# Graph network and mixture of experts on one core: column sums of the late rows in PSUM columns of their own, projections taken earlier, four gate transfers a batch, and the last routing in parts

## The chip, the core and the metric

The kernel runs on one core of a Trainium2 chip. The core has five engines that run side by side and meet only at semaphores: PE (TensorE, matrix products and transposes into PSUM), DVE (VectorE), ACT (ScalarE), POOL (GpSimd) and SP (SyncE, which here only issues transfers). The metric is the device time of one execution in microseconds; lower is better.

## The reference, cut to what matters

```python
# x: (8, 2048, 128), adj: (2048, 2048), 8 experts, the best 2 of them per token
z = layernorm(x)                       # no scale, no shift
A = relu((adj + adj.T) * 0.5)
D = A.sum(axis=1)                      # degrees: row sums of a symmetric matrix
d = where(D > 0, where(D > 0, D, 1) ** -0.5, 0)
x = x + relu((I - d[:, None] * A * d[None, :]) @ (z @ W))
z = layernorm(x)
probs = softmax(z @ router_w.T);  rw, re = top_k(probs, 2);  rw = rw / max(rw.sum(-1), 1e-12)
combine = zeros(N, 8); combine[arange, re] = rw
x = x + z + sum over e of combine[:, e] * (gelu(z @ w1[e] + b1[e]) @ w2[e] + b2[e])
```

All is float32; the kernel splits operands into a high and a low float32r part and makes three products for each one.

## The kernel before, in words

`adj` is cut into 16 x 16 blocks of 128 x 128. Only the lower triangle of the symmetric matrix is kept, in the tile `s_tri` (136 blocks). The program has three stages, and the code of each engine is a list written out by hand; what stands earlier in an engine's list blocks what stands later.

**Setup** walks over the block rows j = 15 down to 0 (r = 0 to 15 in the code, so j = 15 - r). For each row SP loads the row and the column of `adj` (`low`, `up`, in three large buffers and later six half ones; a buffer is loaded again when the row named in `FREED_BY` has been summed). PE transposes the column blocks into PSUM (`turn`), DVE adds the loaded row (`add`, L715), and ACT takes the relu and, with it, the row sums (`relu`, L607). The degrees also need the sums over columns: POOL adds the blocks of rows 14 to 5 into `col_sum` (`add_columns`, L572), and PE turns them into column sums with products of one column (`column_sum`): one with row 15's block, one with `col_sum`, and one for each of the rows 4 to 1 (L671, L675, L679). Between the rows stand 16 jobs of projection: PE transposes a piece of `x` (`turn_x`, L322), ACT copies it (`copy_x`, L328), PE multiplies it by W (`project`, L341) and ACT keeps the result (`keep`, L353), while DVE takes its statistics. The list `JOBS` says how many jobs a row has. `project(k)` waits for `keep(k-2)`, since there are two PSUM buffers. In ACT's list a row's jobs copy ahead of its relus and keep behind them. When the degrees are known in three parts (`degrees`, `root`), ACT and DVE scale the projections into `y_high` (L614) and `y_low` (L742), and the first stage tile is made (`turn_group` L445, `high_group` L452, `low_group` L459).

**Graph** has 32 units (two halves of the batch, 16 block columns each). In a unit PE makes 16 x 3 products of 512 columns (L957 to L959), and between them small work for other units. In the first half units 8 to 15 also carry the projections of the second half, two jobs each. In the second half the operand tile `stage` is read back from DRAM (L861 on SP). Each unit's result is normalised (DVE, POOL), transposed (`turn_z`, L901), split and stored, and routed: PE gives logits, and each four units make one of eight batches, in which DVE picks the best two experts (`pick`, 12 instructions) and weighs them (`weigh`, 10 instructions). The gates then go to DRAM with `store_gates`, 16 transfers a batch (L840). Seven batches are on SP's queue, in units 7, 11, 15, ..., 31, between the loads and stores of the units; the last one is on POOL's.

**Experts** has 32 units of 8 experts. PE makes three products up and three down for each expert (L1317 to L1333), ACT the gelu (L1369) and the high part (L1376), DVE the gate and the low part (L1407, L1412). Its order is software pipelined: `down_product` runs three experts behind. The end of the graph stage's last unit is put between the first experts by `graph_tail`, which looks up the count of experts t in `tail_tensor`, `tail_scalar` and `tail_vector`.

## Time and profile before

| | us |
|---|---|
| median of 3 runs (lowest, highest) | 934.3 (929.2, 935.61) |
| the profiled execution | 933.2 |
| its span (first to last instruction) | 931.5 |
| PE busy | 874.6 (94%) |
| DVE busy | 634.3 (68%) |
| ACT busy | 499.3 (54%) |
| POOL busy | 306.5 (33%) |

The profiled execution took 933.2 us, of which 1.7 lie outside the span. Shares over the span are means over three stages with different limits; the windows of each stage say more. Setup ends and the graph stage begins at 87 us; the experts begin at 539 us.

### The profile page before, as it was taken

Reading aid. Unit: us, or ns where it says so; the run is one execution under the profiler, and the core shown is the slowest. Engines: PE = TensorE matmul, PEld = TensorE weight load, DVE = VectorE, ACT = ScalarE, POOL = GpSimd, SP = SyncE. Lnnn points to the kernel's source line nnn. Section 1 sums busy time; section 2 is a strip of 40 time slices with the busy share of each in tenths; the row PEclk is TensorE's granted clock in tenths of the full one; section 3 lists DMA queues with packets and bytes.
Section 4 is the critical chain, followed back from the end, with each engine's and each line's share of the span. In section 5 each row is a group of like instructions: output and inputs, shape, how many; then the busy total and the mean of one; then the engine's idle time right before and its main releaser. Section 6 shows DMA issues by size and latency. Waiting matters only on the chain.

```text
span 931.5 us, 15186 instructions
## 1 busy us (share of the span) xinstructions
PE 874.6 (94%) x4338; PEld 730.2 (78%) x4338; DVE 634.3 (68%) x1567; ACT 499.3 (54%) x903; POOL 306.5 (33%) x324
## 2 busy tenths in 40 slices
PE   3788999999998999999899988999999999999996
PEld 3688788887786788778687866888888888888885
DVE  3686545657857743252333359999999999999996
ACT  2686423333333311121111168888888888888885
POOL 1792253463664644474244444000000000000000
PEclk9996999999999999999899999999999999999999
DMA  9992366566665356776657865777777777767771
GB/s 284 314 307 104 115 257 260 226 201 215 237 208 196 105 174 248 228 293 219 234 216 284 299 241 176 283 282 276 277 278 280 273 279 271 287 265 279 271 282 51
DMA packets 104477, 222.98 MB, mean 239 GB/s; under 512 B 20888, under 2 KB 71792, under 8 KB 92528
## 3 DMA queue, kind: packets, MB, share of 16 engines
q1 hardware_dynamic: 98848, 212.97, 65.3%
q0 software_dynamic: 3072, 8.59, 2.4%
q10 hardware_dynamic: 2512, 0.86, 0.4%
q8 instruction: 23, 0.38, 0.2%
q14 instruction: 22, 0.18, 0.1%
HBM read 157.89 MB, written 64.49 MB: 239 GB/s over the span
## 4 chain that ended last, share of the span: by engine, by line
PE 61%; issue 12%; POOL 8%; DVE 6%; SPq 5%; DMA 4%; ACT 4%; DVEq 0%; ACTq 0%; POOLq 0%
PE bank L1333 6%; PE bank L1317 6%; PE bank L1319 6%; PE bank L1330 6%; PE bank L1318 6%; PE bank L1331 6%; PE bank L957 5%; PE bank L959 5%; PE bank L958 5%; SPq L840 4%; POOL z L1026 4%; PE bank L341 2%; DMA x_raw<-in_x 2%; POOL rstd L1021 2%; PE bank L1339 1%
## 5 line engine op out<-in xcount | busy, mean ns | idle before, releaser
L1369 ACT ACTIVATE act_h<-bank,b_sb 128x512 f32<-128x512 f32 x256 | 176.2, 689 | 52.2 <-PE bank L1319 47.3
L1407 DVE TENSOR_TENSOR gated<-c_all,act_h 128x512 f32<-128x512 f32 x256 | 176.1, 688 | 33.8 <-ACT act_h L1369 27.9
L1412 DVE TENSOR_TENSOR g_lo<-gated,g_hi 128x512 fp32r<-128x512 f32 x256 | 175.0, 684 | 0.2
L1376 ACT ACTIVATE g_hi<-gated 128x512 fp32r<-128x512 f32 x256 | 159.2, 622 | 4.2 <-DVE gated L1407 4.1
L1301 POOL DMA_DIRECT2D out<-fin x32 | 24.5, 764 | 325.9 <-DVE fin L1420 309.9
L957 PE MATMUL bank<-y,stage 128*128 128x512 f32 x256 | 105.2, 411 | 6.2 <-DMA stage<-s_scratch 6.2
L1021 POOL TENSOR_TENSOR rstd<-var_eps,neg_half 128x4 f32<-128x4 f32 x32 | 48.9, 1527 | 179.0 <-DVE var_eps L1063 178.6
L957 PE MATMUL bank<-y_hi,stage 128*128 128x512 f32 x256 | 107.0, 418 | 0.8 <-DVE y_lo L742 0.8
L1026 POOL TENSOR_SCALAR z<-x,mv,rstd 128x128 f32<-128x128 f32 x128 | 105.2, 837 | 3.4
L978 ACT ACTIVATE z_t<-bank 128x512 f32<-128x512 f32 x32 | 19.1, 598 | 160.9 <-PE bank L901 160.9
L1317 PE MATMUL bank<-z_e,w_hi 128*128 128x512 f32 x256 | 103.3, 403 | 1.4 <-ACT act_h L1369 1.4
L1333 PE MATMUL bank<-g_lo,w_hi 128*128 128x512 f32 x256 | 100.9, 394 | 3.5 <-DVE g_lo L1412 3.5
L959 PE MATMUL bank<-y,stage 128*128 128x512 f32 x256 | 101.6, 397 | 0.0
L959 PE MATMUL bank<-y_hi,stage 128*128 128x512 f32 x256 | 101.2, 395 | 0.0
L958 PE MATMUL bank<-y,stage 128*128 128x512 f32 x256 | 101.2, 395 | 0.0
L1330 PE MATMUL bank<-g_hi,w_lo 128*128 128x512 f32 x256 | 100.6, 393 | 0.0
L1319 PE MATMUL bank<-z_e,w_lo 128*128 128x512 f32 x256 | 100.6, 393 | 0.0
L958 PE MATMUL bank<-y_lo,stage 128*128 128x512 f32 x256 | 100.5, 393 | 0.0
L1331 PE MATMUL bank<-g_hi,w_hi 128*128 128x512 f32 x256 | 100.2, 391 | 0.0
L1318 PE MATMUL bank<-z_e,w_hi 128*128 128x512 f32 x256 | 100.2, 391 | 0.0
L1067 DVE TENSOR_TENSOR z_hl<-z_t,z_hl 128x512 fp32r<-128x512 f32 x32 | 22.2, 693 | 93.5 <-ACT z_hl L981 93.5
L957 PEld LDWEIGHTS bank<-y,stage 128*128 128x128 f32 x256 | 49.2, 192 | 16.6 <-DMA stage<-s_scratch 7.5
(124 smaller groups left out, 1534.2 us busy)
## 6 DMA issues: line engine op xcount, KB each, us to landing
c_all<-c_scratch SPq DMA_DIRECT2D x64, 1024.0 KB, 8.2
s_scratch<-stage SPq DMA_DIRECT2D x14, 2048.0 KB, 8.4
stage<-s_scratch SPq DMA_DIRECT2D x14, 2048.0 KB, 8.5
z_e<-z_scratch SPq DMA_DIRECT2D x32, 512.0 KB, 7.4
z_scratch<-z_hl SPq DMA_DIRECT2D x31, 512.0 KB, 2.7
x_raw<-in_x SPq DMA_DIRECT2D x32, 256.0 KB, 8.2
x_res<-in_x SPq DMA_DIRECT2D x32, 256.0 KB, 7.4
r_e<-res_scratch SPq DMA_DIRECT2D x32, 256.0 KB, 2.7
```

The source lines that it names most:

```text
L957: pe.matmul(out[:, :], s_hi, y_hi, start=(i == 0), stop=False)
L958: pe.matmul(out[:, :], s_hi, y_lo, start=False, stop=False)
L959: last = pe.matmul(out[:, :], s_lo, y_hi, start=False, stop=(i == MB - 1))
L1317: pe.matmul(ps_h[k][:, :], v.w1_hi[:, e, :], v.z_e[s][:, 0, :], start=True, stop=False)
L1318: pe.matmul(ps_h[k][:, :], v.w1_hi[:, e, :], v.z_e[s][:, 1, :], start=False, stop=False)
L1319: pe.matmul(ps_h[k][:, :], v.w1_lo[:, e, :], v.z_e[s][:, 0, :], start=False, stop=True).then_inc(h_done, 1)
L1330: pe.matmul(ps_o[s][:, :], v.w2_lo[:, e, :], hi[:, :], start=False, stop=False)
L1333: pe.matmul(ps_o[s][:, :], v.w2_hi[:, e, :], lo[:, :], start=False, stop=(e == E - 1)).then_inc(o_done, 1)
L1369: act.activation(v.act_h[e % R][:, :], ps_h[e % 2][:, :], ACT.Gelu, bias=v.b1_sb[:, e:e + 1]).then_inc(gelu_done, 1)
L1376: act.activation(v.g_hi[e % R][:, :], v.gated[e % R][:, :], ACT.Copy).then_inc(hi_done, 1)
L1407: dve.tensor_tensor(out=v.gated[e % R][:, :], in0=v.c_all[s][:, e, :], in1=v.act_h[e % R][:, :], op=ALU.mult).then_inc(gated_done, 1)
L1412: dve.tensor_tensor(out=v.g_lo[e % R][:, :], in0=v.gated[e % R][:, :], in1=v.g_hi[e % R][:, :].bitcast(FP32), op=ALU.subtract).then_inc(lo ...
```

## The change

- Setup: `JOBS` takes two projection jobs in rows r = 4 and 5 as well and none in 10 and 11, so that all 16 are issued by the tenth row. The stage tile's first groups move up by one row (r = 11 and 12), and `y_high`'s first ones too.
- Column sums: `LAST` goes from 5 to 9. POOL no longer adds rows 8 to 5; instead each of the rows 8 to 1 gets a one-column product of its own, into its own PSUM column (`row_sums`), and DVE adds up the columns (`deg_col`). The two products with row 15 and `col_sum` are made early (`BASES`).
- Gates: `store_gates` sends four transfers a batch, each with all four units. So that the rows in DRAM are contiguous, the tokens of a unit are stored in another order: `z_hl` is written, and the result read back, through `by_group` and `by_tile`.
- The seam between graph and experts: `turn_z` of the last unit moves from t = 5 to 7, and the last batch's `pick` and `weigh` are cut in eight parts at t = 15, 19, ..., 43. Six units instead of two are written out (`KNOWN`), and POOL stores the last gates behind unit 5.

```diff
-    LAST = 5
-    EARLY_AT = ((15, 14), (13, 12))
-    EARLY = 4
+    LAST = 9
+    EARLY_AT = ((15, 14), (13, 12), (11, 10))
-    JOBS = [2, 2, 2, 2, 1, 1, 1, 1, 1, 1, 1, 1, 0, 0, 0, 0]
+    JOBS = [2, 2, 2, 2, 2, 2, 1, 1, 1, 1, 0, 0, 0, 0, 0, 0]
-    ps_d = [v.banks[2], v.banks[7], v.banks[4]]
+    ps_d = v.banks[2]
+    ps_k = [v.banks[4 if k < 3 else 7][:, k * LAST:(k + 1) * LAST] for k in range(8)]
+    BASES = {8: (7, 6), 9: (5, 4), 10: (3,), 11: (2, 1, 0)}
...
+        def row_sums(j, a, b):
+            pe.wait_ge(relued, until_row(j))
+            for k in range(a, min(j, b)):
+                last = pe.matmul(ps_k[k][:, LAST - j:LAST - j + 1], s_tri[:, block(j, k), :], v.one_col[:, :],
+                                 start=True, stop=True)
+            last.then_inc(row_done, 1)
...
-            if j + 2 < MB:
+            if j + 2 >= 8 and j + 2 < MB:
                 column_sum(j + 2)
-            if r == 12:
+            for k in BASES.get(r, ()):
+                column_sum(k)
+            if 4 <= j + 2 < LAST:
+                row_sums(j + 2, 3, 8)
+            if r == 11:
+                for i in (8, 7, 6):
+                    row_sums(i, 0, 3)
+            if r >= 12:
+                row_sums(j + 2, 0, 3)
+            if r == 10:
                 pr.project(pe, MB - 1)
+            if r == 11:
                 pe.wait_ge(deg_step, 2)
                 pe.wait_ge(pr.hw_kept, MB - 1)
                 for g in range(2):
                     st.turn_group(pe, 0, g)
...
-        column_sum(1)
-        column_sum(0)
+        row_sums(1, 0, 3)
...
+                dve.tensor_reduce(out=v.deg_col[:, a:b], in_=v.banks[7 if p == 1 else 4][:, a * LAST:b * LAST].rearrange(
+                    "p (k i) -> p k i", i=LAST), axis=AX.X, op=ALU.add).then_inc(deg_step, 1)
...
+            if r == 10:
+                dve.wait_ge(pr.xt_copied, MB)
+                dve.memset(v.banks[4][:, 0:3 * LAST], 0.0).then_inc(zeroed, 1)
...
     def store_gates(eng, batch):
         eng.wait_ge(gate_turned, batch + 1)
-        for u in range(4 * batch, 4 * batch + 4):
-            rows = v.c_dram[unit(u)].rearrange("e (q g t) -> g e q t", q=Q, g=4)
-            for g in range(4):
-                eng.dma_start(rows[g], v.gate_x[32 * g:32 * g + 3 * E, Q * (u % 4):Q * (u % 4) + Q, :]).then_inc(
-                    gate_last if batch == U // 4 - 1 else gate_out[half(u)], 16)
+        w = min(unit(4 * batch), unit(4 * batch + 3))
+        rows = v.c_dram[w:w + 4].rearrange("w e (g c) -> g e w c", g=4)
+        for g in range(4):
+            eng.dma_start(rows[g], v.gate_x[32 * g:32 * g + 3 * E, :, :].rearrange(
+                "e (w q) t -> e w (q t)", q=Q)).then_inc(gate_last if batch == U // 4 - 1 else gate_out[half(4 * batch)], 16)
...
-            act.activation(v.z_hl[:, 0, :], v.z_t[:, :], ACT.Copy).then_inc(z_hi_done, 1)
+            act.activation(v.by_group(v.z_hl[:, 0, :]), v.by_tile(v.z_t[:, :]), ACT.Copy).then_inc(z_hi_done, 1)
...
-            act.activation(v.o_t[:, :], ps_o[s][:, :], ACT.Copy).then_inc(ot_copied, 1)
+            act.activation(v.by_tile(v.o_t[:, :]), v.by_group(ps_o[s][:, :]), ACT.Copy).then_inc(ot_copied, 1)
...
-        v.tail_tensor = {5: [(turn_z, U - 1)], 7: [(route, U - 1)]}
+        v.tail_tensor = {7: [(turn_z, U - 1)], 10: [(route, U - 1)]}
-        v.tail_scalar = {6: [(copy_z, U - 1)], 8: [(store_last, U - 1)], 9: [(exps, 7)]}
+        v.tail_scalar = {8: [(copy_z, U - 1)], 12: [(store_last, U - 1)], 17: [(exps, 7)]}
-        v.tail_vector = {6: [(z_low, U - 1)], 8: [(copy_logits, U - 1), (pick, 7)], 10: [(weigh, 7)]}
+        v.tail_vector = {9: [(z_low, U - 1)], 11: [(copy_logits, U - 1)], 15: [(largest, 7, 0)], 19: [(first_of, 7, 0)],
+                         23: [(largest, 7, 1)], 27: [(first_of, 7, 1)], 31: [(add_picked, 7)], 35: [(weigh, 7)],
+                         39: [(split_gate, 7)], 43: [(turn_gates, 7)]}
```

Three places show how instructions move. The first is PE's list from the fifth row's transposes to the seventh's in setup (`up` x11 is row r = 4). Before:

```order
L341 MATMUL bank<-gnn_w_sb,x_t_115 128x128 x4
L662 MATMUL bank<-ident,up_101 128x128 x11
L662 MATMUL bank<-ident,low_100 128x128
L671 MATMUL bank<-one_col,s_tri 128x1
L675 MATMUL bank<-one_col,col_sum 128x1
L322 MATMUL bank<-ident,x_raw_111 128x128 x4
L341 MATMUL bank<-gnn_w_sb,x_t_114 128x128 x4
L662 MATMUL bank<-ident,up_103 128x128 x10
```

The same place with the change (L325 and L344 are `turn_x` and `project`, L673 is `turn`):

```order
L344 MATMUL bank<-gnn_w_sb,x_t_116 128x128 x4
L325 MATMUL bank<-ident,x_raw_112 128x128 x4
L344 MATMUL bank<-gnn_w_sb,x_t_115 128x128 x4
L673 MATMUL bank<-ident,up_101 128x128 x11
L673 MATMUL bank<-ident,low_100 128x128
L683 MATMUL bank<-one_col,s_tri 128x1
L687 MATMUL bank<-one_col,col_sum 128x1
L325 MATMUL bank<-ident,x_raw_113 128x128 x4
L344 MATMUL bank<-gnn_w_sb,x_t_116 128x128 x4
L325 MATMUL bank<-ident,x_raw_114 128x128 x4
L344 MATMUL bank<-gnn_w_sb,x_t_115 128x128 x4
L673 MATMUL bank<-ident,up_103 128x128 x10
```

A second transpose and projection stands ahead of row 4's transposes, and again ahead of row 5's.

The second place is the end of setup on PE, from the last transpose to the first large product. Before:

```order
L662 MATMUL bank<-ident,low_102 128x128
L671 MATMUL bank<-one_col,s_tri 128x1
L675 MATMUL bank<-one_col,col_sum 128x1
L679 MATMUL bank<-one_col,s_tri 128x1 x2
L671 MATMUL bank<-one_col,s_tri 128x1
L675 MATMUL bank<-one_col,col_sum 128x1
L679 MATMUL bank<-one_col,s_tri 128x1 x3
L671 MATMUL bank<-one_col,s_tri 128x1
L675 MATMUL bank<-one_col,col_sum 128x1
L679 MATMUL bank<-one_col,s_tri 128x1 x4
L957 MATMUL bank<-y_hi,stage_96 128x512
```

With the change (L694 is `row_sums`):

```order
L673 MATMUL bank<-ident,up_103 128x128
L673 MATMUL bank<-ident,low_102 128x128
L694 MATMUL bank<-one_col,s_tri 128x1 x3
L673 MATMUL bank<-ident,low_102 128x128
L694 MATMUL bank<-one_col,s_tri 128x1 x3
L999 MATMUL bank<-y_hi,stage_96 128x512
```

Fifteen one-column products behind the last transpose become three. The others stand earlier: behind the transposes of row r = 11 and ahead of the first `turn_group` there are now 18 (six for `BASES` and twelve in a row of `row_sums`, L694), where two stood behind those of row r = 12.

The third place is SP's list in unit 7 of the graph stage, around the first batch of gates. Before:

```order
L269 DMA x_raw_110<-in_x 128x4x128
L269 DMA x_raw_111<-in_x 128x4x128
L840 DMA c_scratch<-gate_x 96x1x32 x16
L869 DMA res_scratch<-res 128x512
L872 DMA z_scratch<-z_hl 128x1024
L853 DMA s_scratch<-stage_96 128x4096
```

With the change:

```order
L272 DMA x_raw_111<-in_x 128x4x128
L272 DMA x_raw_112<-in_x 128x4x128
L882 DMA c_scratch<-gate_x 24x4x128 x4
L911 DMA res_scratch<-res 128x512
L914 DMA z_scratch<-z_hl 128x1024
L895 DMA s_scratch<-stage_96 128x4096
```

Four transfers take the place of sixteen, with the same 96 pieces each, and each piece four times as long.

## Rows read from the trace of the kernel before

**Rows 1.** The page: granted clock of PE in 40 equal slices, in tenths of full speed.

```profile
PEclk9996999999999999999899999999999999999999
```

**Rows 2.** Windows: busy us (x instructions) of PE, PEld, DVE, ACT, POOL; clock, DMA share, GB/s.

```profile
446.00:453.00 7.00, 5.67 (x14) 4.47 (x15) 4.42 (x19) 0.00 (x0) 2.37 (x3) 0.51 1.02 419
...
551.50:555.50 4.00, 4.00 (x12) 3.10 (x12) 1.95 (x3) 2.87 (x5) 0.66 (x1) 0.57 1.01 406
...
600.00:900.00 300.00, 300.00 (x1374) 248.26 (x1373) 274.91 (x441) 259.89 (x441) 19.35 (x26) 1.00 0.75 276
```

**Rows 3.** Timeline of PE in the graph stage: start, us, instruction, idle before it.

```profile
219.28 1.16 PE L341 MATMUL bank<-gnn_w_sb,x_t 128*128 128x128 f32 x8 [1.16 <-ACT x_t L328]
...
286.98 1.16 PE L341 MATMUL bank<-gnn_w_sb,x_t 128*128 128x128 f32 x8 [2.05 <-ACT x_t L328]
...
304.20 1.16 PE L341 MATMUL bank<-gnn_w_sb,x_t 128*128 128x128 f32 x8 [1.54 <-ACT x_t L328]
...
393.22 0.50 PE L957 MATMUL bank<-y,stage 128*128 128x512 f32 x1 [1.22 <-DMA stage<-s_scratch]
...
447.32 0.80 PE L957 MATMUL bank<-y,stage 128*128 128x512 f32 x1 [3.55 <-DMA stage<-s_scratch]
...
500.80 0.80 PE L957 MATMUL bank<-y,stage 128*128 128x512 f32 x1 [1.38 <-DMA stage<-s_scratch]
```

**Rows 4.** Timeline of SP's queue in the graph stage.

```profile
188.48 13.95 SPq L840 DMA_DIRECT2D c_scratch<-gate_x  x16
...
205.10 4.20 SPq L269 DMA_DIRECT2D x_raw<-in_x  x2
...
421.84 13.28 SPq L840 DMA_DIRECT2D c_scratch<-gate_x  x16
...
436.20 0.45 SPq L861 DMA_DIRECT2D stage<-s_scratch  x1
```

**Rows 5.** Timeline of DVE in setup, the adds of rows r = 2 to 5 and 10.

```profile
33.30 2.22 DVE L715 TENSOR_TENSOR s_tri<-bank,low 128x512 f32<-128x512 f32 x4 [3.05 <-PE bank L662]
...
40.50 2.08 DVE L715 TENSOR_TENSOR s_tri<-bank,low 128x512 f32<-128x512 f32 x4 [2.13 <-PE bank L662]
...
46.23 1.89 DVE L715 TENSOR_TENSOR s_tri<-bank,low 128x512 f32<-128x512 f32 x3 [2.22 <-PE bank L662]
49.47 1.74 DVE L715 TENSOR_TENSOR s_tri<-bank,low 128x512 f32<-128x512 f32 x3
...
66.89 1.02 DVE L715 TENSOR_TENSOR s_tri<-bank,low 128x512 f32<-128x512 f32 x2 [0.36 <-PE bank L662]
```

**Rows 6.** Timeline of PE at the end of setup.

```profile
85.37 1.84 PE L679 MATMUL bank<-one_col,s_tri 128*128 128x1 f32 x8
87.07 0.77 PE L957 MATMUL bank<-y_hi,stage 128*128 128x512 f32 x1
```

**Rows 7.** Timeline at the seam: PE, ACT, DVE and POOL.

```profile
550.84 0.65 PE L901 MATMUL bank<-ident,z 128*128 128x128 f32 x4 [3.03 <-POOL z L1026]
...
564.77 0.50 PE L1333 MATMUL bank<-g_lo,w_hi 128*128 128x512 f32 x1 [2.57 <-DVE g_lo L1412]
...
560.05 1.28 ACT L985 ACT_TABLE_LOAD   x1
...
553.11 0.69 DVE L1407 TENSOR_TENSOR gated<-c_all,act_h 128x512 f32<-128x512 f32 x1 [3.61 <-ACT act_h L1369]
...
559.65 0.29 DVE L1084 TENSOR_REDUCE top<-logits 128x16 f32<-128x128 f32 x1
...
563.42 0.69 DVE L1407 TENSOR_TENSOR gated<-c_all,act_h 128x512 f32<-128x512 f32 x1
...
544.10 6.68 POOL L1026 TENSOR_SCALAR z<-x,mv,rstd 128x128 f32<-128x128 f32 x4
```

**Rows 8.** The page: two groups over the whole span: busy us, mean ns of one.

```profile
L1376 ACT ACTIVATE g_hi<-gated 128x512 fp32r<-128x512 f32 x256 | 159.2, 622 | 4.2 <-DVE gated L1407 4.1
...
L1026 POOL TENSOR_SCALAR z<-x,mv,rstd 128x128 f32<-128x128 f32 x128 | 105.2, 837 | 3.4
```

More of the change, by code:

```diff
@@ L586, in gpsimd @@
                     pr.scale_kept(pool, k)
-            if 4 <= r < 12:
+            if r >= 4 and jobs(r):
                 pr.invert(pool, jobs(r))
@@ L666, in column_sum @@
             pe.wait_ge(relued, until_row(MB - 1))
-            if part_of(k) == 2:
-                pe.wait_ge(pr.xt_copied, MB)
-            out = ps_d[part_of(k)][:, k:k + 1]
+            if k in (7, 2):
+                pe.wait_ge(zeroed, 3 if k == 7 else 4)
+            out = ps_d[:, k:k + 1] if k >= 8 else ps_k[k][:, 0:1]
             if k < MB - 1:
@@ L1106, in weigh, with largest @@
-        def weigh(batch):
+        choices = ((v.logits, v.is_1st), (v.others, v.is_2nd))
+        def largest(batch, n):
+            values, k = choices[n][0], STEPS * batch + 6 * n
+            if n == 0:
+                dve.wait_ge(logits_copied, 4 * batch + 4)
+            dve.tensor_reduce(out=v.top[:, :], in_=values[:, :, :], axis=AX.X, op=ALU.max).then_inc(route_step, 1)
+            dve.wait_ge(route_step, k + 1)
+            if n == 0:
+                wait(dve, exp_done, batch)
+                dve.tensor_tensor(out=v.shifted[:, :, :], in0=values[:, :, :], in1=spread(v.top),
+                                  op=ALU.subtract).then_inc(shift_done, 1)
+            dve.tensor_tensor(out=v.same[:, :, :], in0=values[:, :, :], in1=spread(v.top),
+                              op=ALU.is_equal).then_inc(route_step, 1)
@@ new lines, in first_of @@
+        def first_of(batch, n):
+            (values, chosen), k = choices[n], STEPS * batch + 6 * n
+            dve.wait_ge(route_step, k + 2)
+            dve.tensor_tensor(out=v.key[:, :, :], in0=v.same[:, :, :], in1=v.rev_iota[:, :, :],
+                              op=ALU.mult).then_inc(route_step, 1)
+            dve.wait_ge(route_step, k + 3)
+            dve.tensor_reduce(out=v.top_key[:, :], in_=v.key[:, :, :], axis=AX.X, op=ALU.max).then_inc(route_step, 1)
+            dve.wait_ge(route_step, k + 4)
+            dve.tensor_tensor(out=chosen[:, :, :], in0=v.key[:, :, :], in1=spread(v.top_key),
+                              op=ALU.is_equal).then_inc(route_step, 1)
+            dve.wait_ge(route_step, k + 5)
+            if n == 0:
+                dve.scalar_tensor_tensor(out=v.others[:, :, :], in0=chosen[:, :, :], scalar=-3.0e38, in1=values[:, :, :],
+                                         op0=ALU.mult, op1=ALU.add).then_inc(route_step, 1)
+                dve.wait_ge(route_step, k + 6)
@@ L1107, in weigh, with add_picked @@
+        def add_picked(batch):
             first = STEPS * batch + STEPS_A
@@ L1116, in weigh @@
             dve.tensor_reduce(out=v.sum_top[:, :], in_=v.picked[:, :, :], axis=AX.X, op=ALU.add).then_inc(route_step, 1)
+        def weigh(batch):
+            first = STEPS * batch + STEPS_A
             dve.wait_ge(route_step, first + 3)
@@ L1122, in weigh, with split_gate @@
             dve.wait_ge(route_step, first + 5)
+            wait(dve, gate_turned, batch)
+            dve.tensor_tensor(out=v.gate_parts[:, :, 0:E], in0=v.picked[:, :, :], in1=spread(v.inv_top),
+                              op=ALU.mult).then_inc(route_step, 1)
+        def split_gate(batch):
             gate, high, low = (v.gate_parts[:, :, i * E:(i + 1) * E] for i in range(3))
-            wait(dve, gate_turned, batch)
-            dve.tensor_tensor(out=gate, in0=v.picked[:, :, :], in1=spread(v.inv_top), op=ALU.mult).then_inc(route_step, 1)
-            dve.wait_ge(route_step, first + 6)
+            dve.wait_ge(route_step, STEPS * batch + STEPS)
             dve.tensor_copy(high.bitcast(FP32R), gate)
@@ L1132, in weigh, with pick, share @@
             if batch > 4:
-                dve.wait_ge(gate_out[1], 256 * (batch - 4))
+                dve.wait_ge(gate_out[1], 64 * (batch - 4))
             else:
-                wait(dve, gate_out[0], 256 * batch)
+                wait(dve, gate_out[0], 64 * batch)
             dve.transpose(v.gate_x[:, :, :].rearrange("p t c -> p (t c)"),
                           v.gate_parts[:, :, :].rearrange("p t c -> p (t c)")).then_inc(gate_turned, 1)
+        def pick(batch):
+            for n in range(2):
+                largest(batch, n)
+                first_of(batch, n)
+        def share(batch):
+            add_picked(batch)
+            weigh(batch)
+            split_gate(batch)
+            turn_gates(batch)
         for u in range(U):
@@ L1172, in graph_tail @@
 def graph_tail(parts, t):
-    for part, u in parts.get(t, []):
-        part(u)
+    for part, *of in parts.get(t, []):
+        part(*of)
 def expert_stage(nc, sem, v):
@@ L1243, in over_units @@
     def over_units(eng, body):
-        for s in range(2):
-            body(0, s, s)
-        with eng.Fori(1, U // 2) as h:
+        for u in range(KNOWN):
+            body(u // 2, u % 2, u)
+        with eng.Fori(KNOWN // 2, U // 2) as h:
             for s in range(2):
```

98 lines of the change are left out of this document (43 added, 55 removed).

## The prediction

> **What bounds the kernel now.** I read the windows first. From 600 to 900 us PE is busy without a gap at full clock, DVE for 274.9 of the 300 us and ACT for 259.9 [rows 2]. This third of the time can only get longer by the change, so any gain lies before it. The page's clock line [rows 1] has its lowest slice, 6, as the fourth, from 70 to 93 us, and a single 8 near 460; the timeline of PE then shows where it waits. In the graph stage it waits for two things: for an x_t copy of ACT, 1.16, 2.05 and 1.54 us, and for a stage tile that is still being read, 1.22, 3.55 and 1.38 us [rows 3]. SP's queue shows why: the sixteen gate transfers hold it for 13.95 and 13.28 us, and the load of x_raw at 205.10 and the load of the stage tile at 436.20 stand right behind them [rows 4]. At the seam PE waits 3.03 us for POOL's z and 2.57 us for a low part that DVE makes late [rows 7]. In setup no engine is full; the rows follow each other in a chain, and the last thing is PE's own column sums [rows 5, 6].
>
> **Gate transfers.** A batch takes SP 13.95 us for sixteen, 0.87 each; four take 3.5, so 10.4 us of the queue come free in each of seven batches, if a transfer keeps its price. Its pieces are as many as before and four times as long; by the nearest row, the load of a whole stage tile issues in 0.45 us [rows 4], so length doesn't set the price. Bounds: 0.45 to 3.5 us for one, at which nothing would be saved; I take 0.87.
> - Stage loads: the three loads come 10 us earlier, more than the longest wait. All three waits go: 1.22 + 3.55 + 1.38 = 6.15 us.
> - The clock: after the 3.55 us wait the granted clock is 0.51, the lower of the two levels (1.2 GHz), with 5.67 us of PE busy in 7 us [rows 2]. That work takes half as long at the upper level, 2.8 us. A second, shorter such stretch follows the wait at 500.80; its first product takes 0.80 us against a normal one's 0.4 or 0.5, and I put it at 1.6 us. Together 4.4; bounds 0 and 4.4, as nothing else idles PE there.
> - Projections of units 8 to 15: the waits of 1.16 and 2.05 us stand in the units right behind a batch, where x_raw is late. They go: 3.2 us. The 1.54 us wait stands two units behind it, where the pick lies on DVE ahead of the statistics; no SP queue is in it, so it stays. Bounds 1 and 4.75.
>
> The strided writes of z_hl and reads of the result cost nothing in the sum. Their cover is ACT, which idles 40 of 300 us in the experts.
>
> **The seam.** Gone: 3.03 and 2.57 us of waits, and the two stretches at the lower level behind them. The first has 4.00 us of PE busy at a mean clock of 0.57 [rows 2], so 1.7 us; the second I take as equal. In all 5.6 + 3.4 = 9.0 us. New:
> - turn_z comes two experts later. An expert is six products, 300 / 1374 = 0.218 us each, so 1.31 us; two give 2.6 (with the output products some 2.8) against 3.03. Left: 0.3 us.
> - exps moves from beside the pick to t = 17. A table load is 1.28 us, and two with the short exponential make 2.9 us of ACT. PE needs a gelu nine products later, 2.0 us, minus the gelu's own 0.7: 1.3 us of cushion. Left: 1.6 us; bounds 0 and 2.9. It was free before, since it lay in DVE's pick.
> - The pick is 3.8 us (559.65 to 563.42, twelve instructions); ten of weigh at the same price make 3.1. Cut in eight, 0.86 us each four experts. DVE idles 25 of 300 us, 0.44 in four experts, so it falls behind by 0.4 with each piece, 3.4 us at the end. In one piece 3.8 us cost PE 2.57, so DVE's lead is at least 1.2, and the pieces of the pick come first. I take 0.7 us; bounds 0 and 2.2.
> - A stretch at the lower level, 1.7 us, at one in three: 0.6.
>
> New 3.2; net 5.8, bounds 1 and 8.
>
> Here a rule of the Trainium skill, page "ScalarE: Activation LUTs", section "What ACT_TABLE_LOAD costs", speaks against the change: a switch of table costs about 2.66 us with the drain that it brings. The row shows 1.28 us, and the gelu follows. By the page's figure the detour would be 5.6 us instead of 2.9, and the estimate 2.7 us longer.
>
> **Setup.** Here I expect a loss. In the adds of DVE [rows 5], a row with two jobs comes 7.20 us after its forerunner (33.30 to 40.50), a row with one job behind one with two 5.73 (40.50 to 46.23), and a row with one job behind another 3.24 (46.23 to 49.47). The reason is project(k), which waits for keep(k-2): with two jobs in both rows, that keep is behind the last relus. The change makes rows 4 and 5 rows of two. So row 4 comes at 40.50 + 7.20 = 47.7, row 5 at 54.9 instead of 49.47, row 6 at 60.6, and four rows at about 3 give 72.2 for row 10, which stood at 66.89: 5.3 us late. The earlier rows waited for loads at times, and the late ones are then here, so the slip isn't caught up by transfers.
>
> What the end of setup gives back: fifteen one-column products behind the last transpose become three. Four take 1.70 us to the next instruction (85.37 to 87.07) [rows 6], 0.43 each at the lower level: 12 x 0.43 = 5.1 us. But 18 stand now ahead of the first stage groups, 16 more than before; they cost 16 x 0.21 = 3.4 us at the upper level, or 6.9 at the lower. The jobs that left rows 10 and 11 give back something like 1.5 us each that the trace has no row for; bounds 0 and 3. The sum is 5.3 - 5.1 + 3.4 - 1.5 = 2.1 us slower. Bounds: 5 us faster, if the rows catch up and DVE's own chain is all that is left; 7 us slower, at the lower level throughout. Rows 8 to 5 leave POOL's col_sum; POOL is not waited for, so that is worth nothing.
>
> **The sum.** 6.15 + 4.4 + 3.2 + 5.8 - 2.1 = 17.45 us, made against the profiled execution's 933.2: 915.7. The median is 934.3, 1.1 above; I keep 915.5.
>
> **The rivals.**
> - *Setup gains after all* (0.15). The chain of rows is slack I misread, and the tail's 5 us come through whole: 915.5 - 2 - 5 = 908.5. For it: the late rows also waited for loads. Against: the 7.20 and 5.73 us steps.
> - *Setup costs more* (0.15). PE falls to the lower level by row 10, and the 18 products take 6.9 us: 915.5 + 3.5 to 5, or 920. For it: the fourth slice of the clock line is the lowest already [rows 1].
> - *POOL's z is later still* (0.08). POOL took 6.68 us for four of them, 1.67 each, against 0.84 in the mean of the group [rows 7, 8]; DVE was busy up to 549.5 and then idle for 3.61. Without that pause the last 1.28 us of POOL's run would take twice as long, and PE would wait 1.6 instead of 0.3 and fall to the lower level for 1.7: 915.5 + 3 = 918.5. "GPSIMD Engine Reference", section "1. Specifications", of the Trainium skill says the same: GpSimd shares its SBUF interfaces with VectorE, which gets in its way with two SBUF inputs. By that rule it is this rival; the trace agrees with the slowing.
> - *The transfers don't get cheaper* (0.05). If one costs 3.5 us, SP is as full as before: all but the seam and setup falls away, 915.5 + 13.75 = 929. For it: only that no row has a gate transfer of this shape.
> - *Slower than before* (0.03). The copy out of PSUM in another order is in each of the 32 expert units, on ACT. ACT idles 40.1 us in 300, or 1.55 a unit of 11.57 (53 products). A copy of this size takes 0.62 us [rows 8]. If the order of the columns costs it more than 1.55 us extra, PE waits; from 1.55 + 17.7 / 30 = 2.14 us extra, four and a half times the price, the kernel is slower than before. At 3 us extra it is 915.5 + 30 x 1.45 = 959. Nothing in the trace speaks for it.
>
> **How the numbers follow.** My forecast, 915.5 with 911 to 920, has 0.45. The rest, 0.09, is a seam with no new stall, 912. The bounds of the terms reach 4 us below the first rival and 5 above the second: 904 to 925 leaves out the fourth and fifth rival and some tails. What a measurement of this kernel can tell from no change is about 1%, 9.3 us. Faster by more than that, below 925: 0.90. Within it: 0.06. Slower: 0.04.
>
> **What the changed profile would show.** SP: four transfers a batch in 3 to 4 us. PE: no wait for a stage load, and a clock line of 9 from 100 to 540 us. Setup: adds of row r = 5 near 55 us and of row 10 near 72; unit 0's first product at 87 to 90. Seam: a short wait at turn_z, one of 1 to 2 us near t = 20 on ACT's gelu, and no gap of 2.5 us for g_lo. I am wrong if rows 4 to 6 keep their times, if a gate transfer takes over 1.5 us, or if PE waits in the experts after unit 5.

## The result, and the profile after it

The changed kernel takes 925.07 us by the median of 11 executions (920.42 to 928.48), the kernel before 933.9 (924.97 to 936.55, 11 executions). The ratio is 0.992, 95% interval 0.9892 to 0.9947: faster by 0.8%, less than half of what was forecast, and 925.07 stands just outside the range. The profiled execution took 920.42 us (span 918.7), the fastest of the eleven; the number to remember is that the others go up to 928.5 with a lower mean granted clock, 0.977 to 0.985 against its 0.987.

The page of the changed kernel, clock line, which answers to [rows 1]: the dip near 460 us is gone; the 6 of the fourth slice is now two slices of 8.

```profile
PEclk9998899999999999999999999999999999999999
```

Windows of the changed kernel (columns as in [rows 2]). The whole graph stage and the start of the experts run at full clock; the experts take what they took.

```profile
100.00:550.00 450.00, 442.83 (x2268) 369.69 (x2267) 243.89 (x803) 132.69 (x216) 224.87 (x222) 1.00 0.65 233
...
551.50:555.50 4.00, 4.00 (x19) 3.30 (x18) 3.44 (x7) 3.05 (x6) 0.00 (x0) 1.00 0.45 178
600.00:900.00 300.00, 300.00 (x1373) 247.96 (x1372) 275.79 (x443) 259.64 (x441) 21.92 (x30) 1.00 0.75 275
```

SP's queue, the answer to [rows 4]: a batch of gate transfers now holds it for 1.88 to 2.27 us in six of the seven batches and for 4.13 in one, instead of 13.3 to 14.2. No load of a stage tile or of x_raw is waited for, so the waits of [rows 3] on DMA have no successor.

```profile
195.78 2.25 SPq L882 DMA_DIRECT2D c_scratch<-gate_x  x4
...
260.24 4.13 SPq L882 DMA_DIRECT2D c_scratch<-gate_x  x4
...
421.76 1.88 SPq L882 DMA_DIRECT2D c_scratch<-gate_x  x4
431.37 0.33 SPq L903 DMA_DIRECT2D stage<-s_scratch  x1
```

DVE's adds in setup, rows r = 2 to 6 and 10, the answer to [rows 5]. Row 3 starts 0.96 us earlier than before (39.54 for 40.50), and still row 10 comes 7.3 us later (74.18 for 66.89): 8.25 us are lost between the two rows.

```profile
32.34 2.22 DVE L741 TENSOR_TENSOR s_tri<-bank,low 128x512 f32<-128x512 f32 x4 [2.84 <-PE bank L673]
39.54 2.08 DVE L741 TENSOR_TENSOR s_tri<-bank,low 128x512 f32<-128x512 f32 x4 [2.13 <-PE bank L673]
48.71 1.89 DVE L741 TENSOR_TENSOR s_tri<-bank,low 128x512 f32<-128x512 f32 x3 [4.23 <-PE bank L673]
56.07 1.75 DVE L741 TENSOR_TENSOR s_tri<-bank,low 128x512 f32<-128x512 f32 x3 [2.61 <-PE bank L673]
61.41 1.62 DVE L741 TENSOR_TENSOR s_tri<-bank,low 128x512 f32<-128x512 f32 x3 [2.16 <-PE bank L673]
...
74.18 1.02 DVE L741 TENSOR_TENSOR s_tri<-bank,low 128x512 f32<-128x512 f32 x2 [2.02 <-PE bank L673]
```

PE at the end of setup, the answer to [rows 6]. L694 is the new one-column product (two records each): 24 records stand ahead of the first stage group, 24 more between the last transposes, and then PE waits three times for the relus of ACT. The first large product starts at 93.35, not at 87.07, and not at the 87 to 90 of the forecast.

```profile
79.88 2.87 PE L694 MATMUL bank<-one_col,s_tri 128*128 128x1 f32 x24
82.61 1.95 PE L448 MATMUL bank<-ident,s_tri 128*128 128x128 f32 x8
...
85.20 1.52 PE L694 MATMUL bank<-one_col,s_tri 128*128 128x1 f32 x10
...
87.71 0.95 PE L694 MATMUL bank<-one_col,s_tri 128*128 128x1 f32 x8
...
88.78 0.73 PE L694 MATMUL bank<-one_col,s_tri 128*128 128x1 f32 x6
...
90.21 0.61 PE L694 MATMUL bank<-one_col,s_tri 128*128 128x1 f32 x4 [0.54 <-ACT s_tri L617]
91.84 0.38 PE L694 MATMUL bank<-one_col,s_tri 128*128 128x1 f32 x2 [1.02 <-ACT s_tri L617]
93.35 0.80 PE L999 MATMUL bank<-y_hi,stage 128*128 128x512 f32 x1 [1.14 <-ACT s_tri L617]
```

How far PE's own products lie behind ACT's last relu shows in ACT's timeline. These are the ends of the last relu, first in the kernel before, then in the changed one:

```profile
84.06 0.19 ACT L607 ACTIVATION_READ_ACCUMULATOR s_tri<-s_tri 128x1 f32 x1
...
93.11 0.19 ACT L617 ACTIVATION_READ_ACCUMULATOR s_tri<-s_tri 128x1 f32 x1
```

Before, the first large product (87.07) stood 2.8 us behind the end of the last relu (84.25). With the change it stands 0.05 us behind it (93.35 for 93.30).

The seam, the answer to [rows 7]: PE, ACT and POOL. The 2.57 us wait for g_lo is gone; 1.44 us for z are left of 3.03; and a new wait of 1.56 us stands behind the exponential of the last routing. The first POOL line is the unit before the last, whose four z POOL makes while DVE idles.

```profile
542.26 0.66 PE L943 MATMUL bank<-ident,z 128*128 128x128 f32 x4 [1.44 <-POOL z L1068]
...
562.99 0.50 PE L1387 MATMUL bank<-z_e,w_hi 128*128 128x512 f32 x1 [1.56 <-ACT act_h L1439]
...
559.33 1.28 ACT L1027 ACT_TABLE_LOAD   x1
560.62 0.31 ACT L1027 ACTIVATE expo<-shifted 128x128 f32<-128x128 f32 x1
560.95 1.28 ACT L1439 ACT_TABLE_LOAD   x1
562.25 0.69 ACT L1439 ACTIVATE act_h<-bank,b_sb 128x512 f32<-128x512 f32 x1
...
521.72 3.12 POOL L1068 TENSOR_SCALAR z<-x,mv,rstd 128x128 f32<-128x128 f32 x4
534.39 7.81 POOL L1068 TENSOR_SCALAR z<-x,mv,rstd 128x128 f32<-128x128 f32 x4
```

A balance of the two profiled executions: take the large product of unit 0 that waits for DVE's y_lo, at 100.21 before and 107.55 after. Up to it the change lost 7.3 us. From it to the end of the span it won 831.3 - 811.15 = 20.1 us. The forecast had 2.1 lost and 19.55 won. This execution is 4.7 us below the median, so the balance shows less of the loss than the median has.

### The profile page after: what moved, and what is told of

Read it like the earlier page. It is cut to its first block, busy times and chain, and to the rows that moved or that the text cites. A ratio compares the mean times of both kernels' runs of the same rounds, so it can differ in the third digit from the quotient of the medians.

```text
span 918.7 us, 15045 instructions
## 1 busy us (share of the span) xinstructions
PE 872.3 (95%) x4390; PEld 729.6 (79%) x4390; DVE 631.7 (69%) x1571; ACT 499.6 (54%) x903; POOL 292.8 (32%) x306
## 4 chain that ended last, share of the span: by engine, by line
PE 66%; POOL 9%; issue 9%; DVE 7%; ACT 4%; DMA 3%; DVEq 0%; SPq 0%; ACTq 0%; POOLq 0%
PE bank L999 7%; PE bank L1001 7%; PE bank L1000 7%; PE bank L1403 6%; PE bank L1387 6%; PE bank L1389 6%; PE bank L1388 6%; PE bank L1400 6%; PE bank L1401 6%; POOL z L1068 5%; PE bank L344 2%; POOL rstd L1063 2%; ACT s_tri L617 2%; PE bank L950 1%; PE bank L1409 1%
## 5 line engine op out<-in xcount | busy, mean ns | idle before, releaser
L999 PE MATMUL bank<-y,stage 128*128 128x512 f32 x256 | 103.0, 402 | 0.0
L1001 PE MATMUL bank<-y,stage 128*128 128x512 f32 x256 | 100.2, 391 | 0.0
L1000 PE MATMUL bank<-y,stage 128*128 128x512 f32 x256 | 99.7, 389 | 0.0
L1013 ACT ACTIVATE x<-bank,d_out 128x512 f32<-128x512 f32 x32 | 22.0, 689 | 68.7 <-PE bank L1001 68.6
```

Of the source, the lines that this page charges most:

```text
L999: pe.matmul(out[:, :], s_hi, y_hi, start=(i == 0), stop=False)
L1000: pe.matmul(out[:, :], s_hi, y_lo, start=False, stop=False)
L1001: last = pe.matmul(out[:, :], s_lo, y_hi, start=False, stop=(i == MB - 1))
```

## The experiments

All times are medians; the ratio is to the kernel before, run on the same chip. Where two kernels of different chips are compared, it is by their ratios, and a difference of 0.001 is 0.93 us. The intervals of the ratios are 0.0022 to 0.0032 to either side (0.004 for e3 and e8), so a difference of two ratios is known to about 3.4 us, and to 4 or more with e3 or e8.

| kernel | median us | ratio | 95% |
|---|---|---|---|
| changed | 925.07 | 0.992 | 0.9892 to 0.9947 |
| e1 before + gates | 914.55 | 0.9812 | 0.9788 to 0.9837 |
| e2 before + seam | 928.75 | 0.9965 | 0.9943 to 0.9987 |
| e3 before + setup | 946.48 | 1.0162 | 1.012 to 1.0204 |
| e4 changed, old setup | 912.26 | 0.9791 | 0.9767 to 0.9815 |
| e5 e4 + new sums | 917.8 | 0.9858 | 0.983 to 0.9885 |
| e6 e4 + new places of projections | 916.08 | 0.9825 | 0.98 to 0.9849 |
| e7 e4, LAST = 3 | 909.85 | 0.9766 | 0.9739 to 0.9792 |
| e8 changed again | 921.96 | 0.989 | 0.9854 to 0.9926 |
| e9 e7 + fillers in waits | 911.76 | 0.9779 | 0.9749 to 0.9809 |
| e10 e9 + fillers between | 909.04 | 0.9759 | 0.973 to 0.9787 |
| e11 e7, z one expert later | 909.49 | 0.9754 | 0.973 to 0.9779 |
| e12 changed + fillers | 924.27 | 0.9924 | 0.9893 to 0.9956 |

**The three parts, each alone, and setup taken out.** e1 is the gate hunks of the diff shown above, e2 the tables and the split routing, e3 the setup hunks. Their cores:

```diff
e1  -    for g in range(4): eng.dma_start(rows[g], v.gate_x[..., Q * (u % 4):Q * (u % 4) + Q, :])   # per unit
    +    for g in range(4): eng.dma_start(rows[g], v.gate_x[32 * g:32 * g + 3 * E, :, :]...)        # per batch
e2  -        v.tail_tensor = {5: [(turn_z, U - 1)], 7: [(route, U - 1)]}
    +        v.tail_tensor = {7: [(turn_z, U - 1)], 10: [(route, U - 1)]}
e3  -    JOBS = [2, 2, 2, 2, 1, 1, 1, 1, 1, 1, 1, 1, 0, 0, 0, 0]
    +    JOBS = [2, 2, 2, 2, 2, 2, 1, 1, 1, 1, 0, 0, 0, 0, 0, 0]
    -    LAST = 5
    +    LAST = 9
```

> The kernel before with only the gate part of the change: four transfers a batch, the logits of units placed in the order of the units in memory, and the permuted copies of z and of the output that go with it. Theory A (the setup edit is what ate the gain): the stage-load waits of rows 3 go, and the lower-clock stretches after them, so 11 to 14 us less than the kernel before, 920 to 923 us by medians. Rival B (the forecast's graph terms were too large, and the profiled execution of the changed kernel was a lucky one): 3 to 7 us less, 927 to 931 us.

> The kernel before with only the seam part: later places in the tables of the last unit's work, the last routing on VectorE in parts, six expert units written out, the last gate stores on GpSimd behind unit 5. Its gate stores are still 16 transfers a batch. Theory A: of the 9.0 us of waits and lower clock at the seam 5 to 6 us are gained, 928 to 929 us. Rival B: the waits of the changed trace at the seam (1.39, 1.44 and 1.56 us) take nearly all of it, 1 to 2 us gained, 932 to 933 us.

> The kernel before with only the setup part: row sums in PSUM columns of their own, two projections a row through row 5, the first stage groups a row earlier. Theory A: unit 0's products start 7.3 us later and nothing behind them gains from it, except the 3.2 us of waits on late projections in the graph's first units: 3 to 7 us slower than before, 937 to 941 us. Rival B (the setup edit pays, and the loss lies elsewhere): 0 to 3 us faster, 931 to 934 us.

> The changed kernel with the setup of the kernel before: gate and seam parts kept. Theory A: the first products come 7.3 us earlier than in the changed kernel, of which the waits on late projections in the graph's first units (3.2 us) are taken back: 4 to 7 us less than the changed kernel, 918 to 921 us. Rival B: the late projections put the graph behind again, and its time is that of the changed kernel within 1 us, or above it.

Measured by ratio: gates 17.5 us faster, seam 3.3 us faster, setup 15.1 us slower, and gates and seam together (e4) 19.5 us faster. e4 is what the forecast had for these two, 19.55. So the setup edit costs the changed kernel 12.0 us (0.9791 to 0.992), nearly six times the 2.1 of the forecast. Both sides of my expectations were too small: e1 passed its theory's 14, e3 its 7, and e4 came at 912.26 where 918 to 921 were expected. e2 met its theory A.

PE of e3 shows the lost time. Its first two lines are from the timeline, the rest from windows of PE, PEld, DVE, ACT, POOL, clock, DMA share and GB/s:

```profile
82.82 5.26 PE L692 MATMUL bank<-one_col,s_tri 128*128 128x1 f32 x24
...
100.53 0.79 PE L992 MATMUL bank<-y_hi,stage 128*128 128x512 f32 x1 [1.14 <-ACT s_tri L615]
...
74.00:92.00 18.00, 18.00 (x99) 18.00 (x98) 5.39 (x15) 6.41 (x23) 1.64 (x1) 0.57 0.03 7
92.00:104.00 12.00, 10.86 (x45) 10.10 (x45) 8.31 (x24) 7.39 (x17) 2.17 (x3) 0.50 0.27 111
```

The same windows of the kernel before:

```profile
74.00:92.00 18.00, 17.61 (x76) 16.59 (x77) 11.29 (x28) 11.38 (x28) 2.41 (x4) 0.53 0.37 132
92.00:104.00 12.00, 11.24 (x57) 8.94 (x56) 8.72 (x16) 7.55 (x13) 0.00 (x0) 1.00 0.10 44
```

In the kernel before, the stretch at the lower level (1.2 GHz) goes from 74 to near 91 us; in e3 it goes from about 77 to 103, and its first large product comes 13.5 us later than the 87.07 of [rows 6]. The 24 records take 5.26 us there, 0.22 each; in the profiled execution of the changed kernel the same 24 took 2.87, since its clock came back to the upper level (2.4 GHz) for a while.

**Setup taken apart: e5 and e6**, both from e4.

```diff
e5  -    ps_d = [v.banks[2], v.banks[7], v.banks[4]]
    +    ps_k = [v.banks[4 if k < 3 else 7][:, k * LAST:(k + 1) * LAST] for k in range(8)]
    +            if 4 <= j + 2 < LAST: row_sums(j + 2, 3, 8)
    +            if r == 13:
    +                for i in (8, 7, 6, 5): row_sums(i, 0, 3)
e6  -    JOBS = [2, 2, 2, 2, 1, 1, 1, 1, 1, 1, 1, 1, 0, 0, 0, 0]
    +    JOBS = [2, 2, 2, 2, 2, 2, 1, 1, 1, 1, 0, 0, 0, 0, 0, 0]
    -            if r == 12:
    +            if r == 11:      # first stage groups; the others a row earlier too
```

> The old-setup version of the changed kernel (e4) with the new column sums alone: the setup's projections keep the old places, 2, 2, 2, 2, 1 and so on, and the stage groups theirs; rows 8 to 1 of the matrix are summed by one-column products into PSUM columns of their own, 36 products instead of 10. Theory S (the products are the cost): 26 more products are 52 more records of 0.11 us at full clock to 0.21 us at half clock, 5.5 to 11 us on TensorE, which waits for little there: 918 to 923 us against e4's 912.3. Rival J (the doubled rows 4 and 5 are the cost, the products run in gaps): within 2 us of e4.

> The old-setup version of the changed kernel (e4) with the new places of the projections alone: two a row through row 5, the last by row 10, the first stage groups from row 11; the column sums stay as before. Theory S: two more waits of about 2.2 us for the kept projection in rows 4 and 5, less the 2.4 us wait that stood before the stage groups and what two later rows lose; 911 to 915 us. Rival J: the late rows 4 and 5 carry through to the first product, 5 us late, 917 us or more.

The sums cost 6.2 us (0.9791 to 0.9858), the places of the projections 3.2 (to 0.9825), which is at the edge of what these runs can tell from nothing. Together 9.4 of the 12.0; the rest, 2.6, is inside the uncertainty. e8 below, the changed kernel on the chip of e5 and e6, has 0.989, 9.2 us above e4, and by it nothing is left over. In e5 theory S held: 917.8 us is just below its 918 to 923 and not within 2 us of e4. (Its profiled execution, the fastest of six, is only 3.4 us above e4's.) e6, at 916.08, fell between its theory's 911 to 915 and its rival's 917 or more, and decides nothing between them. PE of e5 has 32 of the new records in one piece ahead of a stage group, and behind all of them still waits for ACT's relu:

```profile
77.69 5.01 PE L690 MATMUL bank<-one_col,s_tri 128*128 128x1 f32 x32
82.57 1.73 PE L448 MATMUL bank<-ident,s_tri 128*128 128x128 f32 x7
...
89.10 0.79 PE L993 MATMUL bank<-y_hi,stage 128*128 128x512 f32 x1 [1.92 <-ACT s_tri L614]
```

Its first large product comes at 89.10 against e4's 86.39, though only three products stand behind the last transpose, as in the changed kernel. The way from row 3's adds on DVE to row 10's is 28.42 us in e5 and 26.27 in e4, and the last relu ends 5.5 us later, at 89.05 for 83.57. PE makes the new products ahead of later rows' transposes, so they delay the rows; of the 5.5 us, 2.8 come back because fewer products stand at the end. In e6 the first large product came at 92.38, in an execution that was the slowest of its five.

**Fewer products instead of more: e7.**

```diff
-    LAST = 5
+    LAST = 3
```

> The old-setup version of the changed kernel (e4) with one number changed: GpSimd adds rows down to 3 instead of 5 into its column sums, so the one-column products at the end of the setup fall from 10 to 3. Theory S run the other way: 7 products of two records of 0.21 us at the lower clock leave TensorE at the place where it waits for nothing, 3.0 us less, 909 to 910 us, if GpSimd's two more additions come in time. Rival (the end of the setup is bound by VectorE's and ScalarE's last rows, TensorE merely fills): within 1 us of e4.

2.3 us less than e4 by ratio, under the uncertainty, in the direction and near the size of theory S. The trace says what limits it: in e4 the first large product stands 2.8 us behind the end of the last relu (86.39 for 83.57), in e7 0.05 us (85.39 for 85.34), and PE now waits for ACT's relu, if only 0.18 us. So the relus end last, the seven products were worth 2.8 us at most, and no further product taken off PE would help. In this execution the relus themselves ended 1.8 us later than in e4's, so the first product is only 1.0 us earlier.

```profile
84.22 0.99 PE L681 MATMUL bank<-one_col,s_tri 128*128 128x1 f32 x4
85.39 0.80 PE L964 MATMUL bank<-y_hi,stage 128*128 128x512 f32 x1 [0.18 <-ACT s_tri L609]
```

**The changed kernel once more: e8.**

> The changed kernel once more, to see an execution near its median. Theory: the profiled one of the first look, 920.4 us with a mean granted clock of 0.987, missed most of the lower-clock stretch that the setup-only version shows from 76 to 103 us; this one, at 0.978 or so, has it, and its first large product comes at 97 to 100 us instead of 93.35. Rival: the difference lies elsewhere in the span, as short stretches in the graph or the expert part.

At 922.19 us and a clock of 0.985 this was again no execution of 925 or more. Its first large product is at 95.17, between the 93.35 of the first profiled execution and the 97 to 100 of the theory. Added up from 42 to 108 us, PE is at the lower level for about 17 us in the kernel before, in e4 and in the 920.42 us execution of the changed kernel, for 20 in e8 and for 34 in e3. Which work the executions of 925 us or more have at the lower level was not seen; e3's long stretch is the nearest evidence.

**Holding the clock: e9, e10 and e12.** The extra products write PSUM columns that nobody reads.

```diff
e9  +        def fill(bank, n):
    +            for _ in range(n):
    +                pe.matmul(v.banks[bank][:, :], ident[:, :], v.x_t[(MB - 1) % 2][:, :], start=True, stop=True)
    +                fill(4, 2)      # r == 12, ahead of the first stage groups
    +                fill(4, 1)      # r == 13, ahead of the next
e10 +                fill(5, 1)      # r == 14, 15, and between column_sum(1) and column_sum(0)
e12 +                fill(4, 32) twice in r == 11, fill(5, 0) in each row from 12   # in the changed kernel
```

> The version with ten products made three (e7), with three extra products of 512 columns in TensorE's two waits around the first stage groups (1.54 and 1.44 us in e7): two ahead of the first groups, one ahead of the next. Their results are not used. Theory C (the wait is what takes the clock down near 78 us): the clock stays at the upper level through the one-column products that follow, some 5 us of busy time there and 3 us of the first large products cost half, 3 to 4 us less than e7: 906 us. Rival D (the clock falls with the one-column products, whatever stands ahead of them, as in the changed kernel at 76 us with no wait over 0.3 us ahead of it): no gain, 910 to 912 us, the last from fillers that run over.

> As e9, with three more extra products of 512 columns between the one-column products of the last two rows and ahead of the last column's. Their results are not used. Each costs about 1 us at the upper level, 3 us in all, on TensorE's busy stretch. Theory C: nothing more to win, so 3 us over e9. Rival D: the clock now stays at the upper level up to the first large product, the one-column products and the first large ones cost 4 to 6 us less, and the fillers give 3 back: 907 to 909 us, 1 to 3 below e9.

> The changed kernel with six extra products of about 512 columns among the one-column products from row 11 on, two in row 11 and one in each later row. Their results are not used. They cost about 0.95 us each at the upper level, 5.7 us in all. The old-setup version (e4) was 12.8 us below the changed kernel; the new sums alone cost 5.0 and the new places of the projections alone 3.3 of that, so 4.5 us appear only with both together. Theory L (that rest is the lower clock on a longer busy stretch): the clock holds through most of it, the one-column products take half as long and the fillers give back what they cost; 918 to 923 us, with a mean granted clock of 0.985 or more in each execution. Rival (the rest is the rows' lateness, on ACT and VectorE, whatever the clock): the six products add to TensorE's path or fill waits, 925 to 931 us.

In e9 the clock fell all the same, near 81 us, behind the one-column products of the last rows. But PE waits there too, since the fillers had only shortened the earlier waits, to 0.63 and 0.42 us, and the last relus were still to come:

```profile
81.11 0.59 PE L681 MATMUL bank<-one_col,s_tri 128*128 128x1 f32 x2 [0.70 <-ACT s_tri L609]
83.80 0.79 PE L970 MATMUL bank<-y_hi,stage 128*128 128x512 f32 x1 [2.11 <-ACT s_tri L609]
```

In e10, with large products between the one-column ones, the clock stayed at the upper level up to 84 us and fell there, behind a wait of 0.55 us; it came back near 87, as in e9. PE, windows as above:

```profile
72.00:84.00 12.00, 10.46 (x59) 7.04 (x58) 6.25 (x15) 8.26 (x27) 3.84 (x5) 1.00 0.05 23
84.00:90.00 6.00, 6.00 (x22) 4.55 (x21) 5.16 (x13) 3.90 (x7) 1.89 (x3) 0.72 0.94 339
```

and e7 without them:

```profile
72.00:84.00 12.00, 9.02 (x58) 8.78 (x57) 6.46 (x17) 8.07 (x25) 5.50 (x5) 0.75 0.01 4
84.00:90.00 6.00, 5.82 (x23) 4.87 (x23) 5.38 (x18) 2.96 (x7) 2.18 (x3) 0.65 0.78 306
```

Both times fell where rival D had them (911.76 in 910 to 912, 909.04 in 907 to 909), and the clock stayed up longer in e10 as it said. What takes the clock down isn't shown by that: in e9 the fall came with a new wait of 0.70 us, and in e10 it came too, 3 us later. The worth is small. By ratio e9 is 1.2 us above e7 and e10 0.7 below, both inside the uncertainty. e10's first large product comes at 83.43 us, 1.96 earlier than e7's but only 0.37 earlier than e9's, and waits 0.55 us for ACT's relu. It is the chain of rows that ends last there, and a faster PE wins little. e12 took 924.27 us where 918 to 923 and 925 to 931 were expected: by ratio it is the changed kernel. The clock did not hold in each execution, as theory L asked: seven of the ten took 920.6 to 925.2 us at 0.986 to 0.990, the other three 927.8 to 931.7 at 0.977 to 0.980. Its profiled execution has the upper level from 90 us on, but six products in the way, and its first large product at 98.18. That the lower clock is what keeps the changed kernel from e4 was not shown by it.

**The seam: e11.**

```diff
-        v.tail_tensor = {7: [(turn_z, U - 1)], 10: [(route, U - 1)]}
+        v.tail_tensor = {8: [(turn_z, U - 1)], 11: [(route, U - 1)]}
```

(copy_z goes from 8 to 9, z_low from 9 to 10, copy_logits from 11 to 12.)

> The version with ten products made three (e7), with the last unit's turn of z, its copy and the routing product each one expert later in the tables (turn 8 instead of 7, and so on); the rest of the tables stays. Theory Z (the 1.44 us wait on GpSimd's z is what the forecast's seam term missed): one expert is 1.31 us, the wait falls to 0.1 to 0.2 us, 1.3 us less: 908.5 us. Rival: the wait moves to the products that need the last unit's z or logits, within 0.5 us of e7.

The 1.44 us wait on z is gone from the timeline of PE, and nothing took its place: from the first wait in the experts to the last g_lo that is waited for, PE takes 375.21 us (524.02 to 899.23) against e7's 376.34 (523.17 to 899.51), 1.1 less. That agrees with theory Z. The times alone don't decide: the ratio is 1.1 us below e7's and the median 0.4, less than a measurement tells. The wait behind the exponential stays:

```profile
524.02 0.50 PE L1352 MATMUL bank<-z_e,w_hi 128*128 128x512 f32 x1 [1.39 <-ACT act_h L1404]
553.03 0.50 PE L1352 MATMUL bank<-z_e,w_hi 128*128 128x512 f32 x1 [1.57 <-ACT act_h L1404]
```

e11, with the old setup, LAST = 3 and the later z, has the lowest ratio, 0.9754, some 15 us below the changed kernel; e10, e7 and e9 are within the uncertainty of it.

## Why the prediction was wrong

**Gate transfers: the mechanism right, the size 3.7 us too small.** 13.75 us were forecast, 17.5 measured (e1). All three waits for a stage tile went, and the lower clock behind them. A wait on z of 0.83 us stands at 414.82 before and at 406.55 in e1, and the first wait in the experts at 542.27 and 524.42 (no rows above show these). Between the two the lead of e1 grows from 8.27 to 17.85, by 9.6 us: 3.55 + 1.38 of waits, and 4.65 where 4.4 stood in the forecast for the clock. The undersized term is that of the projections: it took two waits, 1.16 and 2.05 us, and the graph's first half won 6.8 us up to the wait that [rows 3] have at 304.20 (297.45 in e1), with a wait of 0.79 us on x_raw and one of 0.53 on x_t gone as well; the last 2.2 us went in pieces that no row here accounts for. The wait of 1.54 us that was to stay stayed, 1.52. A gate transfer costs about 0.5 us (1.0 in one batch), not the 0.87 of sixteen, inside the bounds.

**The seam: 5.8 forecast, 3.3 measured (e2).** The exponential's detour was taken as 1.6 us and is 1.56. The pieces of the routing, 0.7 us in the forecast, show one wait on g_lo, 0.20 us at 586.08, and no stretch at the lower level came, 0.6 in the forecast. The z was mis-sized: 0.3 us were to be left, 1.44 are. That was the rival "POOL's z is later still", but for its stretch at the lower level, which did not come: with the moved tables DVE has work through most of the stretch, and POOL's four z take 7.81 us, 1.95 each, where the four of the unit before, with DVE idle, take 3.12. "GPSIMD Engine Reference", section "1. Specifications", of the Trainium skill gives a reason: GpSimd's SBUF interfaces are shared with VectorE, and a VectorE instruction with two SBUF inputs contends for them. DVE's products and differences there (gated, g_lo) are of that kind, and the trace agrees with the slowing; no run here took DVE's work away at that place to show the cause. The other page cited ahead, "ScalarE: Activation LUTs", would have had the detour at 5.6 us; the load took 1.28 us both times, the gelu began 0.02 us behind it, and PE waited 1.56. The z explains 1.1 of the 2.5 us that were missed; from the first wait in the experts to the last g_lo waited for, the changed kernel takes 376.53 us for 380.71 before, 4.2 less. What holds the rest isn't known, and e2's interval, 2 us to either side, could take most of it. Two sizes that missed on opposite sides made gates and seam together 19.5, by luck what was forecast.

**Setup: the step that failed.** The forecast lost 2.1 us there; 12.0 were lost by ratio. What failed is its account of the one-column products: it left 22 of the 26 new ones out of the sum, and it priced the tail at PE's whole time, though only 2.8 us of it lay behind the other engines. Term by term:
- *"What the end of setup gives back: fifteen one-column products behind the last transpose become three ... 12 x 0.43 = 5.1 us."* It gives back 2.8 us. Before, ACT's last relu ended at 84.25, so PE's products held the first large one back only from there to 87.07; the rest of them ran while the relus were still to come. With the change the relu ends at 93.30, and PE waits 0.54, 1.02 and 1.14 us for the last relus. e5 has the same 2.8, and e7, with seven products fewer, reached the same limit.
- *"But 18 stand now ahead of the first stage groups, 16 more than before."* True, and not the whole count. The profile's page has 4390 PE instructions for 4338, 52 more; a product is two records, so 26 products are new, and 12 fewer at one place and 16 more at another account for 4. The other 22 stand elsewhere in rows r = 8 to 14, unpriced. At 0.11 us a record (upper level) to 0.22 (lower) they are 5 to 10 us on PE. The whole sums part was forecast at 1.7 us gained, and e5 measured 6.2 lost.
- *Rows 4 and 5 with two jobs: 5.3 late, less 1.5.* The mechanism held. Row 4 came at 48.71 and row 5 at 56.07, steps of 9.17 and 7.36 for the 7.20 taken twice. In the first of them PE was at the lower level from 45 to 48.4 us, behind a wait of 2.44 us for the kept projection; that the wait took the clock down isn't shown, since the kernel before and e3 have the same wait with the clock at the upper level from 44 to 48 (e3's step is 7.65). From row 3 to row 10 the slip is 8.25 us; by e5 about 2.1 of it are the new products' (28.42 - 26.27), which leaves some 6 for the jobs. 3.8 us was forecast for this part and 3.2 measured by ratio (e6), though the profiled execution of e6, the slowest of its five, took 918.1 us, 5.7 over e4's 912.43, with its first large product 6.0 us later.

So in the profiled execution the last relu is 9.05 us late (93.30 for 84.25), the tail gives 2.8 back, and the first large product is 6.3 late; at the product that waits for y_lo it is 7.3. The median is 4.7 us above this execution, and no profile shows where those lie.

**The rivals.** "Setup costs more" was nearest. Its reason, the lower level by row 10, was seen in e3, while in the profiled changed kernel the 24 records of the large group ran mostly at the upper level; its 3.5 to 5 us on top of 2.1 were half of what came. "Setup gains after all", at equal odds with it, counted on 5 us from a tail of which 2.8 could be had. The range's upper end, 925, was 5 us above the 920 of the first of these. None of the prediction's three signs of being wrong came: rows 4 to 6 were late, a gate transfer took less than 1.5 us, and PE's waits in the experts after unit 5 are those of the kernel before. They would not have caught this error; the place forecast for the first large product, 87 to 90 us, did.

**What stays open.** Whether the lower clock adds anything to the 9.4 us of e5 and e6; by e8's ratio nothing is left for it, by the first eleven executions 2.6 us. What takes the clock down in the late rows: long stretches of one-column products went with it in e3, but no run separates them from the rest. And what an execution of the changed kernel at 925 to 928 us has at the lower level; a mean clock of 0.979 for 0.987 is, as an estimate from these two means, some 15 us more of it.

## What to carry to other kernels

When a sum is rearranged, count all its instructions over the whole stage, and let the instruction count on the profile's page be the check: a difference of counts at two places isn't the difference of the work. Before a tail of one engine is priced as a gain, ask which engine's work ends last once it is gone; here ACT's last relu ended 2.8 us ahead of PE's products, and no more than that could be won of 5.1. And for an edit in three parts, measure each part: the kernel without the setup part is 12 us faster than the whole.

## What the runs showed of the hardware

- A gate transfer with pieces four times as long held its queue for less time, not more: sixteen took 13.3 to 14.2 us, 0.83 to 0.89 each, and four took 1.88 to 2.27, about 0.5 each, in six batches and 4.13 in one.
- A product of one column took PE 0.23 us at the upper level and 0.43 at the lower (24 records from 79.88 to 82.61 in the changed kernel, from 82.82 to 87.94 in e3; a product is two records). The large products, of 512 columns and one record each, start 0.22 us apart at the upper level (1374 in 300 us, [rows 2]). So a one-column product is no cheaper than one of them.
- Dozens of one-column products, between small transposes, went with the lower clock though PE did not wait: in e3 the clock fell near 77 us and stayed down to 103, with PE busy for 18.00 us of the 18 from 74 to 92. That they are the cause isn't shown.
- GpSimd's four z took 3.12 us with DVE idle and 7.81 us with DVE busy, in neighbouring units of the changed kernel.
- The same kernel's executions spread by 8 us, the longer ones mostly at a lower mean granted clock: 920.4 us at 0.987, 928.5 at 0.978. The old-setup version, with fewer one-column products, spread by 3.5 us (910.16 to 913.65, 0.983 to 0.988).
